# Sums scattered into the second routing's order, and hidden tiles read by plain loads

## What is computed

```python
def _route_dense(z, k, tau):
    topi = jax.lax.top_k(z, k)[1]
    topv = jnp.take_along_axis(z, topi, axis=1)
    w = jax.nn.softmax(topv / (tau + EPS), axis=1)
    ...
def _apply_mixture(x, dw, W):
    y = jnp.zeros((x.shape[0], W.shape[1]), x.dtype)
    for e in range(W.shape[0]):
        y = y + x @ W[e].T * dw[:, e:e + 1]
    return y
...
x_addr = x_flat @ P_w.T
dw1 = _route_dense(x_addr @ U1.T, K, TAU)      # K = 3
dw2 = _route_dense(x_addr @ U2.T, K, TAU)
dw3 = _route_dense(x_addr @ U3.T, K, TAU)
h = _apply_mixture(x_flat, dw1, W1)            # 256 -> 1024
h = jax.nn.gelu(h, approximate=False)
y = _apply_mixture(h, dw2, W2)                 # 1024 -> 256
y = y + dw3 @ b2
```

## Time and profile before

| | us |
|---|---|
| median of 3 runs | 1221.43 |
| lowest, highest | 1219.93, 1226.13 |
| span of the profiled execution | 1216.9 |
| PE busy in it | 1094.3 (90%) |
| POOL busy in it | 381.8 (31%) |
| expansion c = 0 | about 610 to 733 |
| expansion c = 1 | about 733 to 840 |
| contraction, 118 halves | 849 to 1187 |
| the end | 1187 to 1216.9 |

### The profile page before, as it was taken

How to read it: one execution, slowest core, us unless ns; L and a number is a source line. 1 busy time by engine, 2 the same in 40 slices (tenths; PEclk the granted TensorE clock), 3 DMA queues, 4 the chain that set the end, 5 groups by cost and what they waited for, 6 DMA issues and landing times.

```text
span 1216.9 us, 19171 instructions
## 1 busy us (share of the span) xinstructions
PE 1094.3 (90%) x6013; PEld 817.2 (67%) x6013; DVE 552.3 (45%) x1120; ACT 420.3 (35%) x833; POOL 381.8 (31%) x421
## 2 busy tenths in 40 slices
PE   7999899998999999999399999998677888888885
PEld 4888744888998878887244443444566777776773
DVE  4988766764444446776872501333122211111114
ACT  1566544321112225664244432332222232222220
POOL 0221100000220011011154434552666646665650
PEclk8999999998999999999599999998898899999998
DMA  7000130004980029001155578997778865444437
GB/s 208 2 0 0 33 139 1 1 1 161 345 286 9 0 66 382 27 0 47 37 180 200 186 211 295 349 364 276 249 253 278 269 201 179 134 131 142 132 121 281
DMA packets 93410, 187.89 MB, mean 154 GB/s; under 512 B 14109, under 2 KB 34575, under 8 KB 93340
## 3 DMA queue, kind: packets, MB, share of 16 engines
q1 hardware_dynamic: 65346, 109.45, 25.4%
q0 software_dynamic: 23696, 73.69, 19.6%
q10 hardware_dynamic: 4298, 3.81, 1.0%
HBM read 133.56 MB, written 55.44 MB: 155 GB/s over the span
## 4 chain that ended last, share of the span: by engine, by line
PE 40%; issue 4%; DMA 4%; DVE 2%; another core or an unknown queue 2%; ACT 1%; SPq 0%; POOL 0%; POOLq 0%; DVEq 0%; ACTq 0%
PE f_psY L2089 18%; PE f_psH L2046 15%; PE f_psV L2072 4%; DMA W<-in_f_W1T 2%; DMA W<-p_d 2%; PE f_psT L2034 1%; ACT a_W L2146 1%; DVE W L1650 1%; PE f_psV L83 1%; DMA shared<-h_d,f_half_toks 0%; PE f_psH L1929 0%; PE f_psV L1662 0%; SPq L2343 0%; DVE f_xTk L2268 0%
## 5 line engine op out<-in xcount | busy, mean ns | idle before, releaser
L2089 PE MATMUL f_psY<-W,a_W 128*128 x944 | 240.7, 401 | 57.4 <-issue 35.6
L2089 PEld LDWEIGHTS f_psY<-W,a_W 128*128 128x128 f32 x944 | 179.4, 200 | 87.0 <-issue 65.4
L2046 PE MATMUL f_psH<-W,f_xTk 128*128 x472 | 215.5, 596 | 5.7 <-ACT shared L2141 2.0
L2046 PEld LDWEIGHTS f_psH<-W,f_xTk 128*128 128x128 f32 x472 | 84.1, 190 | 96.0 <-issue 95.6
L2146 ACT ACTIVATE a_W<-f_psV 128x512 f32<-128x512 f32 x118 | 70.0, 598 | 155.8 <-PE f_psV L2072 94.8
L2141 ACT ACTIVATE shared<-f_psH 128x512 f32<-128x512 f32 x118 | 70.4, 597 | 142.1 <-PE f_psH L2046 109.5
L1692 POOL DMA_INDIRECT W<-p_d,f_rows x96 | 95.0, 989 | 64.7 <-issue 24.7
L1692 POOL DMA_INDIRECT shared<-h_d,f_half_toks x90 | 87.6, 974 | 85.4 <-DMA p_d<-shared 25.6
L2246 DVE TENSOR_SCALAR a_W<-W,f_wt 128x512 f32<-128x512 f32 x32 | 15.9, 496 | 204.7 <-DMA W<-p_d,f_rows 147.6
L2268 DVE TENSOR_TENSOR f_xTk<-f_psY,f_xTk 128x256 f32<-128x256 f32 x52 | 21.7, 424 | 144.1 <-PE f_psY L2089 112.5
L1692 POOL DMA_INDIRECT a_W<-xn_d,f_toks x59 | 57.6, 975 | 88.9 <-PE f_psT L2034 54.3
(11 more groups left out here) (299 smaller groups left out, 1867.8 us busy)
## 6 DMA issues: line engine op xcount, KB each, us to landing
p_d<-shared SPq DMA_DIRECT2D x118, 256.0 KB
W<-in_f_W1T SPq DMA_DIRECT2D x24, 512.0 KB, 8.8
W<-in_f_W2T SPq DMA_DIRECT2D x24, 512.0 KB
m_wg<-in_m_Wg SPq DMA_DIRECT2D x16, 512.0 KB, 4.0
m_wu<-in_m_Wu SPq DMA_DIRECT2D x16, 512.0 KB, 5.2
m_wd<-in_m_Wd SPq DMA_DIRECT2D x16, 512.0 KB, 6.1
h_d<-a_W SPq DMA_DIRECT2D x32, 256.0 KB
W<-p_d SPq DMA_DIRECT2D x16, 384.0 KB, 9.2
```

The costliest lines, as they stand in the source:

```text
L2046: mm = pe.matmul(psH[:, n % 2, :], xTk[:, i, k, :], W1[c][:, e, k, :], start=k == 0, stop=k == KD - 1)
L2089: mm = pe.matmul(psY[:, n % 2, 0:D], hT[:, m % 2, k, :], W2[c][:, e, k, :], start=k == 0 and not (whole and c == 1), stop=k == KQ - 1 and ...
```

## The change

The sum of a token tile is no longer stored in token order. POOL scatters it three times, by the token's three places in the second routing's sorted order (`scatter_sum`), into `hs_d`, one tensor per half. A hidden tile of the contraction is then a plain block of 128 rows, and SP loads it (`load_hidden`), after all scatters of its half have landed. All 59 tiles run in two rounds, c = 0 and then c = 1; the tiles done in both halves at once, the table of turns and `half_toks` go. POOL's wait for `h_mm` in the sums for c = 0 goes too. The gathers and scatters of the sums stand in one sequence per half, the results' scatters after both. W2's parts 0 to 6 of the first half are loaded during the expansion, parts 7 to 11 behind the first seven hidden tiles, the second half's among the hidden tiles. Since padding rows of `hs_d` are written by nobody, both tensors (2 x 7552 rows of 2 KB) are filled with finite numbers from W1 in the first attention (`fill_sorted_rows`); the 4 MB fill of `h_d` goes.

```diff
+        def fill_sorted_rows(sp):
+            rows = t["f_W1T"].rearrange("e k (c h) -> (e k c) h", c=2)
+            n = rows.shape[0]
+            for c in range(2):
+                sp.dma_start(hs_rows[c][0:n, :], rows).then_inc(hs_filled, 16)
+                sp.dma_start(hs_rows[c][n:LT * P, :], rows[0:LT * P - n, :]).then_inc(hs_filled, 16)
...
-                            all_products(0)
-                            for u in range(TT):
-                                if u >= GR:
-                                    pool.wait_ge(h_mm, LT + SPACE * u)
-                                for k in range(TOP):
-                                    three(u, k)
-
-                            all_products(1)
-                            all_sums(0)
-                            for n in range(QUAD):
-                                hidden(n)
-                            done, spread_over = QUAD, FIRST - QUAD - LATE
-                            for r in range(TT * TOP):
-                                three(TT + r // TOP, r % TOP)
-                                while (done - QUAD) * TT * TOP < (r + 1) * spread_over:
-                                    hidden(done)
-                                    done += 1
-                            for n in range(done, FIRST):
-                                hidden(n)
-                            all_sums(1)
-                            for n in range(FIRST, len(turns)):
-                                hidden(n)
-                                if n >= FIRST + DEEP - 1:
-                                    scatter(n - DEEP + 1)
-                            for n in range(len(turns) - DEEP + 1, len(turns)):
-                                scatter(n)
+                            def gather_picks(u):
+                                c, i = divmod(u, TT)
+                                for k in range(TOP):
+                                    fetch(pool, g[c][:, u % GR, k, :], p1_rows[c], rows[:, 0, k, i:i + 1], g_ld[u % GR])
+
+                            def scatter_sum(u):
+                                c, i = divmod(u, TT)
+                                pool.wait_ge(hs_ready, u + 1)
+                                for k in range(TOP):
+                                    pool.indirect_dma_start(
+                                        hs_rows[c], bass.IndirectOffsetOnAxis(ap=rows[:, 1, k, i:i + 1], axis=0),
+                                        hs[:, u % 2, :], None).then_inc(hs_scattered[u % 2], 16)
+
+                            pool.wait_ge(list_ready, 1)
+                            pool.wait_ge(hs_filled, 16 * N_FILL)
+                            for c in range(2):
+                                all_products(c)
+                                for i in range(GR):
+                                    gather_picks(c * TT + i)
+                                for i in range(TT):
+                                    scatter_sum(c * TT + i)
+                                    if i + GR < TT:
+                                        gather_picks(c * TT + i + GR)
+                            for i in range(LT):
+                                pool.wait_ge(yo_ready, i + 1)
...
                             def combine(u):
                                 i = u % TT
                                 dve.wait_ge(g_ld[u % GR], 16 * TOP * (u // GR + 1))
-                                wait(dve, hs_stored[u % 2], 16 * (u // 2))
+                                wait(dve, hs_scattered[u % 2], 16 * TOP * (u // 2))
...
+                            for e in range(AHEAD, EARLY):
+                                load_w2(0, e)
+                            for s in range(QUAD):
+                                sp.wait_ge(po_stored[s], landed(2 * LT, s, QUAD))
+
+                            def load_hidden(m):
+                                c, i = divmod(m, LT)
+                                if i == 0:
+                                    for s in range(2):
+                                        sp.wait_ge(hs_scattered[s], 16 * TOP * (c + 1) * TT // 2)
+                                if m == QUAD:
+                                    sp.wait_ge(b_mm, TT)
+                                wait(sp, hT_mm, m - DEEP + 1)
+                                sp.dma_start(hg[m % DEEP], hs_d[c][i]).then_inc(hg_ld[m % DEEP], 16)
+
+                            for c in range(2):
+                                for i in range(DEEP):
+                                    load_hidden(c * LT + i)
+                                for e in range(EARLY, E1):
+                                    load_w2(c, e)
+                                for i in range(DEEP, LT):
+                                    load_hidden(c * LT + i)
+                                    if c == 0 and i % W2_STEP == 0 and i // W2_STEP - 2 in range(EARLY):
+                                        load_w2(1, i // W2_STEP - 2)
```

More of the change, by code:

```diff
@@ L1 @@
-from collections import namedtuple
 from contextlib import ExitStack, contextmanager
@@ L59 @@
 DEEP = 7
-WHOLE = 7
-LATE = 4
 TT = B * NT
@@ L548, in attention, with _ @@
                 with nc.Block() as block:
-                    if not first:
+                    if first:
+                        @block.sync
+                        def _(sp):
+                            fill_sorted_rows(sp)
+                    else:
                         @block.sync
@@ L1676, in found_tokens @@
                         one.step(dve.tensor_tensor(pair[:, :], pair[:, :], own[:, :], ALU.add))
[L1677 to L1683, removed]
+                        one.step(dve.tensor_copy(pairi[:, :], pair[:, :]))
+                        one.step(dve.tensor_copy(dest[:, :], pairi[:, :]))
                 spent = att[1][0][:, :, :, :].rearrange("p w k d -> p (w k d)")
@@ L1696, in tokens @@
                     wait(pool, xgT_mm, i - QUAD + 1)
-                    fetch(pool, xg[:, i % QUAD, :], xn_d, toks[:, 0, i:i + 1], xg_ld[i % QUAD])
+                    fetch(pool, xg[:, i % QUAD, :], xn_d, toks[:, i:i + 1], xg_ld[i % QUAD])
                 SUMS = 2 * TT
[L1700 to L1718, removed]
-                            freed[a] = half + n
-                        turns.append(Turn(kind, i, seats[0], used[seats[0]], free, half))
-                        half += n
-                    assert sorted(u.tile for u in turns if u.kind != "second") == list(range(LT))
-                    assert half == 2 * LT
-                    return turns
-                turns = turns_of_products()
-                halves_of = [(n, c) for n, u in enumerate(turns) for c in ((0, 1) if u.kind == "whole" else (int(u.kind == "second"),))]
-                TILES = len(halves_of)
+                TILES = 2 * LT
                 def landed(n, slot, ring):
@@ L1974, in hidden @@
-                            def hidden(n):
-                                u = turns[n]
-                                wait(pool, hT_mm, u.free)
-                                if u.kind == "first" and u.tile == QUAD:
-                                    pool.wait_ge(b_mm, TT)
-                                if u.kind == "whole":
-                                    fetch(pool, sel[:, 0:HID], h_rows, toks[:, 1, u.tile:u.tile + 1], hg_ld[u.seat])
-                                else:
-                                    c = int(u.kind == "second")
-                                    fetch(pool, hg[u.seat], h_half, half_toks[:, c, u.tile:u.tile + 1], hg_ld[u.seat])
@@ new lines, in _ @@
+                            for i in range(QUAD, LT):
+                                tokens(pool, i)
+                            pool.wait_ge(list_ready, 1)
[8 more added lines that the diff above has]
+                                        gather_picks(c * TT + i + GR)
@@ L2205, in _ @@
                             lists(dve, one, psN)
+                            one.step(dve.tensor_copy(rows[:, 1], pki[:, :, :]))
                             owners(dve, one, 1)
```

110 lines of the change are left out of this document (34 added, 76 removed).

## The result

The changed kernel takes 1351.89 us (median; 1347.0 to 1354.7) and the kernel before, beside it, 1222.64 us: a ratio of 1.106 (95% interval 1.102 to 1.110). It is 10.6% slower. The profiled execution has a span of 1351.7 us.

The account below looks back on a forecast made before the run. Expansion was taken as PE-bound; contraction lost 83 of 338 us to counts held by POOL's runs. Expansion to 915 (+75), second run to 1056, 97 halves to 1266, end 30: span 1296; with 4.5 more, 1300 us, range 1180 to 1360.

Parts of the forecast that it names:

- likeliest case: Whole kernel: one PE count passes per 2 to 7 us during POOL's long runs; 1300 us, 1235 to 1350, chance 0.50.
- C: Both POOL runs: no counts pass after the first 9 to 14 us; 1390 us, chance 0.10 including what lies between.
- two outer bounds: Slowest values allowed: expansion c=1 +110 us, and 11 us a half (12 halves) during the second POOL run.
- Counts held back by unbroken runs: Sums: long unbroken runs of POOL's indirect DMAs delay PE's counts until POOL's service, at 1.44 us an issue, catches up.
- One run of 96: Sums c=0: POOL issues 96 gathers and scatters without pausing, 120 us at 1.25 or 138 at 1.44; 138 taken.
- One count per 4 us: Expansion c=1 during POOL's first run: PE's counts pass at this pace, ending expansion at 915, +75 us (+15 to +110).
- 6.4 us a half in the second run, 21 halves: First contraction during sums c=1: this pace from 924 until POOL's run ends at 1056; bounds 4 and 11 us.
- 2.165 us a half after that: Rest of the contraction after POOL's second run: 97 undisturbed halves take 210 us, to 1266.
- The end: From 1187 to the span's end in the kernel before: 30 us, unchanged.
- A: Sums: long runs hold PE no more than short ones, or POOL pauses; faster, 1177 to 1210 us, chance 0.28.
- B: Faster case plus 0.46 us an issue lost in expansion, or W2 loads 10 late: no difference, 1215 to 1228, chance 0.12.
- the prediction's D: Both round starts: the last of three scattered copies land late when DMA is full, 5 to 10 us each; no separate chance.

Follow-up runs that it names:

- The rests: The changed kernel with a POOL rest of some 1.2 us after every three indirect DMAs: 1234.61 us, 1.012 of the kernel before; 1235.88 and 1234.89 in other sets.
- held level: No change of code: sets of runs in which the kernel before had a median of 1220 to 1224 us.
- free level: No change of code: sets of runs in which the kernel before had a median of 1160.6 or 1161.5 us.

## Why the prediction was right, and where its terms were off

The forecast was slower, 1300 us, by one mechanism; the time is 1351.9, inside the range of 1180 to 1360, near its end. Sign and mechanism were right, the size was not: 1351.9 lies just outside the likeliest case's own range (1235 to 1350). The pace that came, one count per 10.5 to 12 us, isn't in the case that had 0.50 (one per 2 to 7 us) but in what had 0.10 (C and what lies between). With its two outer bounds, +110 us and 11 us a half, the prediction's steps give about 1350 of span, so the time is the worst that it had allowed for short of C. That the wide range holds it is in part luck. Step by step:

- **Counts held back by unbroken runs**: right. It is the step on which the rest stands, and it was read from one stall of 9 us and two smaller ones. The rests settle it for the held level: broken runs with the same bytes cost nothing of it. At the free level the step would have failed, since runs of over 90 issues held nothing there.
- **One run of 96, 120 to 138 us**: right. From 735.00 to 859.66, and counts come again at 867.94; the second run from 937.59 to 1063.2, counts at 1072.95. No pause for DVE's sums.
- **One count per 4 us**: mis-sized. It was one per 10.5 to 12, which I had as the outer bound. I had taken a value between gaps of short runs; but short runs show only how the hold begins. The one long enough to show it whole, the 17 issues of the earlier trace rows, had said 10.73. Expansion c = 1 ended at 934 and not at 915: +94.5 us where +75 was forecast and +110 was the bound.
- **6.4 us a half in the second run, 21 halves**: the term that failed most. Seven halves started. 6.4 was the mean of three halves of which two fell before the hold set in. Two counts at 11 us make 22 us a half, and 28 to 34 were seen: ACT's starts on them, from 982.49 to 1061.03, are by turns 10.5 to 12 and 22.5 us apart. Why every second gap is double stays open. 14 halves more for later, at 2.165 us, are 30 us.
- **2.165 us a half after that**: nearly. 111 halves from 1074.02 to 1322 take 248 us, 2.235 each. The piece of five W2 parts in the second round, which I had put at nothing here, took PE from its tiles once, for 3.16 us, at 1205.60, and its next eight matmuls ran at the lower clock.
- **The end**: 1322 to 1351.7, 29.7 us, as forecast.

With the three terms at their measured size the sum is 1296 + 19 + 30 + 8 = 1353, against 1351.7.

Of the rivals, A (a long run holds no more than short ones) and B are out in the held sets: PE stayed at 1.72 us a tile for six tiles only. C, the total loss, was near in size but not in kind, since one count passed per 11 us. The landing scatters of the prediction's D cost nothing at the start of the first round: SP's first load of a hidden tile was issued at 939.76, long after the sequence had ended at 859.66, and PE began on the tile 6.4 us later. The Trainium skill ("DMA: Bandwidth & Descriptors", "Issuing engines are not separate DMA queues") has it that DMAs of every engine share the same 16 DMA engines and that issuing on several saves only issue time. The free sets fit that: 78 issues of POOL stood beside a full PE. In the held sets the trace shows a loss beyond it: a count of PE, whose matmuls had ended at 852.9, came at 867.9, with the DMA share at 0.00 from 862 on.

One thing the reading couldn't know: it holds for the level at which the trace before was taken. In a free set the kernel before is 61 us shorter, so that most of the 83 us which it explained aren't there.

No version beat the kernel before. The one with tied waits and spread parts of W2 is level where nothing is held and 0.7% slower where it is. What would remain to be tried is both at once, short rests and W2 spread.

## What to carry to other kernels

Look at how many indirect DMAs POOL issues in a row and not only at how busy it is: a wait that spaces them may be what keeps TensorE running. In the held sets a rest of about 1.2 us after every three did that with no tie to anything; in the free ones there was nothing to gain by it. Where a stall has two sizes in a trace, take the price of a long stretch from the longest run in it, not from the mean. And read the time of the kernel before beside every experiment: here the same kernel stood at two levels 5% apart, and an experiment at the wrong level answers nothing.

## What was unexpected of the hardware

- In the held sets PE's counts come late while a long run of POOL's lasts: one per 10.5 to 12 us reaches ACT, and the last of them come when 1.385 to 1.42 us per issue have passed from the run's start, or some us later, even when the DMA engines are idle (share 0.00) and POOL too. DVE's and the DMAs' own counts came through meanwhile: the sums kept pace with POOL over all 96 issues.
- Whether that happens changes from set to set, 1161 or 1222 us for the same kernel, and not with the chip. Within a set the executions of the kernel before agreed to 0.8%. The cause is open.
- In a free set a run of over 90 of the same issues held nothing: PE was busy for 110.00 of 110 us beside 78 of them and 362 GB/s.
- Three issues per 5 us hold back no counts at either level (1235 us at both).
- 30.9 MB of copies within DRAM ran in the first attention, in slices of 311 to 340 GB/s, and cost nothing that can be seen: PE was busy for 90.7 us of the first 101, before the change for 91.4, and the first sequence began at 735.00 against 738.67.
